# A second iteration written out for each engine, with single context units and the value products ahead of the Toeplitz products

## The reference, cut to what matters

```python
def layernorm(x): return (x - mean(x)) / sqrt(var(x) + 1e-5)
# 1: mixing by Toeplitz matrices, 16 heads of 16 columns
z = softmax(layernorm(x) @ W_A.T / 4, over the rows)         # (512, 16)
v = layernorm(x) @ W_V.T
mix[i, h] = sum over j <= i of z[i - j, h] * v[j, h]         # (512, 256)
x = x + mix @ W_O.T + b_O
# 2: causal attention of the rows on a context given from outside
K, V, Q = ctx @ WK, ctx @ WV, layernorm(x) @ WQ
x = x + softmax(mask(Q @ K.T / 16)) @ V
# 3: a feed-forward part with 2 shared and 16 routed experts, top 2
x = x + shared(layernorm(x)) + routed(layernorm(x))
```

## Time and profile before

| | |
|---|---|
| median of 3 runs | 574.45 us (573.6 to 577.08) |
| the profiled execution | 573.51 us |
| its span, first to last instruction | 571.7 us |
| TensorE busy | 541.9 us, 95% of the span |
| DVE busy | 426.5 us, 75% |
| ScalarE busy | 255.7 us, 45% |
| POOL busy | 191.8 us, 34% |
| TensorE's granted clock | 1.00 throughout |

### The profile page before, as it was taken

How to read it: one execution, slowest core, us unless ns; L and a number is a source line. 1 busy time by engine, 2 the same in 40 slices (tenths; PEclk the granted TensorE clock), 3 DMA queues, 4 the chain that set the end, 5 groups by cost and what they waited for, 6 DMA issues and landing times. The chain is left out here.

```text
span 571.7 us, 12923 instructions
## 1 busy us (share of the span) xinstructions
PE 541.9 (95%) x4716; PEld 368.2 (64%) x4716; DVE 426.5 (75%) x1107; ACT 255.7 (45%) x517; POOL 191.8 (34%) x240
## 2 busy tenths in 40 slices
PE   5787889999999999999999999999999998999997
PEld 4565557566685667766786668666866675666455
DVE  5858687868885787868886888778876776677654
ACT  4565546445354254445344445434543334332332
POOL 4215150223542144223522343234421343133123
PEclk9999999999999999999999999999999999999999
DMA  8995595795439903694449743993189125300351
GB/s 256 308 367 194 182 386 180 155 322 183 112 82 251 335 17 101 148 292 151 111 100 249 242 110 77 204 310 98 51 177 325 57 74 126 64 1 1 86 102 37
DMA packets 90734, 94.70 MB, mean 166 GB/s; under 512 B 28224, under 2 KB 76224, under 8 KB 90432
## 3 DMA queue, kind: packets, MB, share of 16 engines
q1 hardware_dynamic: 90688, 94.09, 58.1%
HBM read 75.66 MB, written 12.12 MB: 154 GB/s over the span
## 5 line engine op out<-in xcount | busy, mean ns | idle before, releaser
L694 POOL TENSOR_TENSOR mid<-gated,mid 128x512 f16<-128x512 f32 x72 | 86.6, 1202 | 214.0 <-ACT mid L880 213.9
L880 ACT ACTIVATE mid<-gated 128x512 f16<-128x512 f32 x72 | 44.9, 624 | 83.3 <-DVEq L1225 80.0
L146 PE MATMUL wide<-w_d,mid 128*128 128x256 f16 x288 | 78.5, 273 | 0.0
L148 PE MATMUL wide<-w_d,mid 128*128 128x256 f16 x288 | 78.5, 273 | 0.0
L147 PE MATMUL wide<-w_d,mid 128*128 128x256 f16 x288 | 78.5, 272 | 0.0
L1203 DVE SCALAR_TENSOR_TENSOR gated<-gated,score 128x512 f32<-128x512 f32 x72 | 49.1, 682 | 37.6 <-ACT gated L875 37.5
L146 PE MATMUL rows<-h3T,w_gu 128*128 128x512 f16 x160 | 60.7, 379 | 0.3 <-DVEq L126 0.3
L146 PE MATMUL score<-h3T,w_gu 128*128 128x512 f16 x160 | 60.7, 379 | 0.2
L147 PE MATMUL rows<-h3T,w_gu 128*128 128x512 f16 x160 | 60.6, 379 | 0.0
L148 PE MATMUL rows<-h3T,w_gu 128*128 128x512 f16 x160 | 60.6, 379 | 0.0
L148 PE MATMUL score<-h3T,w_gu 128*128 128x512 f16 x160 | 60.6, 379 | 0.0
(11 more groups left out here) (249 smaller groups left out, 1402.8 us busy)
## 6 DMA issues: line engine op xcount, KB each, us to landing
toep<-z_scratch SPq DMA_DIRECT2D x14, 2048.0 KB, 18.3
stage<-comb_scratch SPq DMA_DIRECT2D x32, 512.0 KB, 8.5
toep<-z_scratch SPq DMA_DIRECT2D x4, 1024.0 KB, 11.2
x_bo<-in_x SPq DMA_DIRECT2D x8, 512.0 KB, 11.8
x_in<-in_xr SPq DMA_DIRECT2D x7, 512.0 KB, 11.1
qT<-q_scratch SPq DMA_DIRECT2D x7, 512.0 KB, 3.9
vx<-v_scratch SPq DMA_DIRECT2D x7, 512.0 KB, 5.2
out<-x_out SPq DMA_DIRECT2D x7, 512.0 KB, 3.0
```

Source lines behind the costliest of these rows:

```text
L146: pe.matmul(out, stationary[0], moving[0], start=start, stop=False, **kw)
L148: return pe.matmul(out, stationary[1], moving[0], start=False, stop=stop, **kw)
L694: pool.tensor_tensor(mid_slot(j, 1, late), gate_slot(j, late), mid_slot(j, 0, late), ALU.subtract).then_inc(mid_split.sem, 1)
L880: act.activation(mid_slot(j, 0, late), gate_slot(j, late), ACT.Copy).then_inc(mid_hi.sem, 1)
```

## The change

The second iteration leaves the shared `iteration` functions and gets a function of its own, `second_iteration`, on POOL, ScalarE, DVE and TensorE. The tables `CONTEXT_AT` and `CONTEXT_BEFORE` go. The operations are the same, but for these points:

- TensorE makes both value products ahead of the Toeplitz products. Both units (1,2), (1,3) come after the mix turn, units (2,0) to (2,2) ahead of the h2 turn, and the others singly between the steps of the attention; the last two end the iteration, behind the turn of h1.
- The two gate pieces that were last on DVE (numbers `GATES_2` and `GATES_2 + 1`) are made later, and their low half on POOL: a multiplication in place (`w_scaled`) and a subtraction, where DVE used one instruction. ScalarE copies them behind h2T and behind the second exponent, and waits for them one by one.
- The normalisation of x_in for block 2 goes from DVE to ScalarE (`normalise_x`), with its shift made by POOL (`make_shift_x`); the counters' offset is changed to match.
- z's maximum comes earlier on DVE, and x_in's statistics are made in two halves between the attention's steps.
- POOL's list is now: bias, context 2, reciprocal and shift for h2, context 3, the two pieces, context 4, reciprocal and shift for x_in, context 5, the two reciprocals for h3.
- SP loads the residual of block 0 and context 2 ahead of the second gate weights.

In the diff below, the removed branches `if first:` of the shared functions are left out, and `project_mix` loses its second argument.

```diff
--- before.py
+++ after.py
@@ -62,10 +62,6 @@
-CONTEXT_AT = {5: (4, (0, 1)), 6: (4, (2, 3)), 7: (5, (0, 1)), 8: (5, (2,))}
-CONTEXT_BEFORE = {3: (3, (2,)), 4: (3, (3,))}
@@ -280,6 +276,9 @@
...
+        LATE = len(pieces) - LATE_PIECES
+        GATES_2 = LATE - 2
@@ -607,9 +607,10 @@
                 if f and not m:
 
                     sp.wait_ge(first_toep_loaded, 32)
+                    load_residual(it)
+                    load_context(2)
                     load_gates(1)
-                    load_context(2)
-                if f and not d:
+                if f and m and not d:
                     load_residual(it)
                 if f and not m:
                     load_context(3)
@@ -712,8 +713,37 @@
...
+            def part_weights(some):
+                for i in some:
+                    n, k, at = pieces[i]
+                    name, _, dst, _, _ = loads[n]
+                    pool.wait_ge(w_hi, i + 1)
+                    pool.wait_ge(w_lo, i)
+                    src = staged[name][:, k, at]
+                    pool.tensor_scalar(src, src, X_W, None, ALU.mult).then_inc(w_scaled, 1)
+                    pool.wait_ge(w_scaled, i - GATES_2 + 1)
+                    pool.tensor_tensor(dst[:, 1, k, at], src, dst[:, 0, k, at], ALU.subtract).then_inc(w_lo, 1)
+            def second_iteration(it):
+                add_bias(it - 1)
+                part_context_columns(2)
+                reciprocal_deviation(it - 1, 1)
+                make_shift(it - 1)
+                part_context_columns(3)
+                part_weights(range(GATES_2, LATE))
+                part_context_columns(4)
+                reciprocal_deviation(it + 1, 0)
+                make_shift_x(it + 1)
+                part_context_columns(5)
+                reciprocal_deviation(it - 1, 2)
+                reciprocal_deviation(it - 1, 2, 1)
+                if f and m and not d:
+                    second_iteration(it)
+                    return
@@ -925,11 +949,59 @@
...
+            def second_iteration(it):
+                part_context(1, (0, 1))
+                part_weights(range(MIDDLE, GATES_2))
+                for g in range(K2):
+                    take_first_mix(g)
+                part_values(it, it, 0)
+                part_values(it, it, 2)
+                part_turned(it, it - 1, mixT, mixT_hi, "mix")
+                part_context_columns(2)
+                part_context(1, (2, 3))
+                z_powers(it)
+                act.wait_ge(w_lo, GATES_2)
+                part_context(2, (0,))
+                part_context_columns(3)
+                part_context(2, (1,))
+                normalise_last(it - 1, it)
+                part_context(2, (2,))
+                part_turned(it, it - 1, h2T, h2T_hi, "h2")
+                part_weights(range(GATES_2, GATES_2 + 1))
+                part_context(2, (3,))
+                part_z(it)
+                part_context(3, (0,))
+                exp_scores(it, it - 1, 0)
+                exp_scores(it, it - 1, 1)
+                part_weights(range(GATES_2 + 1, LATE))
+                part_context(3, (1,))
+                act.wait_ge(ctx_stored[1], 32)
+                part_prob(it, it - 1, 0)
+                exp_scores(it, it - 1, 2)
+                part_context_columns(4)
+                act.wait_ge(w_lo, GATES_2 + 1)
+                part_context(3, (2,))
+                part_prob(it, it - 1, 1)
+                exp_scores(it, it - 1, 3)
+                part_context(3, (3,))
+                part_prob(it, it - 1, 2)
+                part_context(4, (0,))
+                part_prob(it, it - 1, 3)
+                part_context_columns(5)
+                part_context(4, (1,))
+                act.wait_ge(w_lo, LATE)
+                part_context(4, (2, 3))
+                normalise_x(it + 1)
+                part_turned(it, it - 1, h3T, h3T_hi, "h3")
+                part_context(5, (0, 1))
+                part_turned(it, it + 1, h1T, h1T_hi, "h1")
+                part_context(5, (2, 3))
+                if f and m and not d:
+                    second_iteration(it)
+                    return
@@ -1339,12 +1377,93 @@
...
+            def add_residual(it, k):
+                if not k:
+                    dve.wait_ge(x_biased.sem, x_biased.at(it - 1, 1))
+                    dve.wait_ge(x_kept.sem, x_kept.at(it - 2, 1))
+                rows.take(dve, it, f"o{k}")
+                dve.wait_ge(rows.ready.sem, rows.is_ready(it, f"o{k}"))
+                dve.scalar_tensor_tensor(x_res[:, k:k + 2], rows.bank(f"o{k}")[:].rearrange("p (c e) -> p c e", c=2),
+                                         1 / (X_MIX * X_W), x_bo[:, k:k + 2], ALU.mult,
+                                         ALU.add).then_inc(rows.taken.sem, 1)
+                hold(dve, rows.taken, rows.is_taken(it, f"o{k}"))
+                return statistics(1, x_res, range(k, k + 2))
+            def attended_statistics(it, c):
+                hold(dve, turned.taken, turned.is_taken(it, f"p{c}"))
+                return statistics(2, x_res, [c])
+            def second_iteration(it):
+                b = it - 1
+                rows.take(dve, it, "v0")
+                part_context(1, (0, 1))
+                part_weights(range(MIDDLE, GATES_2))
+                z_max(it)
+                part_values(it, it, 0)
+                part_values(it, it, 2)
+                rows.take(dve, it, "o0")
+                part_turned(it, b, mixT, mixT_hi, "mix")
+                turned.take(dve, it, "h2.0")
+                part_context(1, (2, 3))
+                add_residual(it, 0)
+                aggregate(b, 1, add_residual(it, 2))
+                part_context(2, (0,))
+                normalise(b, it, 1, x_res, h2)
+                z_invert(it)
+                score.take(dve, it, "s0")
+                part_context(2, (1, 2))
+                part_turned(it, b, h2T, h2T_hi, "h2")
+                part_context(2, (3,))
+                part_z(it)
+                part_context(3, (0,))
+                for c in range(2):
+                    score_max(it, b, c)
+                for c in range(2):
+                    score_sum(it, b, c)
+                score.take(dve, it, "s2")
+                part_context(3, (1,))
+                part_prob(it, b, 0)
+                x_statistics(it + 1, range(2))
+                score_max(it, b, 2)
+                score_sum(it, b, 2)
+                score.take(dve, it, "s3")
+                part_context(3, (2,))
+                part_prob(it, b, 1)
+                attended(it, 0)
+                score_max(it, b, 3)
+                score_sum(it, b, 3)
+                attended_statistics(it, 0)
+                part_context(3, (3,))
+                part_prob(it, b, 2)
+                attended(it, 1)
+                x_statistics(it + 1, range(2, C))
+                part_context(4, (0,))
+                part_prob(it, b, 3)
+                aggregate(b, 2, attended_statistics(it, 1))
+                attended(it, 2)
+                part_context(4, (1,))
+                normalise(b, it, 2, x_res, h3)
+                attended(it, 3)
+                attended_statistics(it, 2)
+                aggregate(b, 2, attended_statistics(it, 3), 1)
+                part_context(4, (2,))
+                normalise(b, it, 2, x_res, h3, 1)
+                part_context(4, (3,))
+                for banks in (score, rows):
+                    banks.reach(dve, banks.taken, it)
+                part_turned(it, b, h3T, h3T_hi, "h3")
+                part_context(5, (0, 1))
+                part_turned(it, it + 1, h1T, h1T_hi, "h1")
+                part_context(5, (2, 3))
+                turned.reach(dve, turned.taken, it)
@@ -1745,38 +1827,72 @@
...
+            def second_iteration(it):
+                b = it - 1
+                pe.wait_ge(turned.taken.sem, turned.is_taken(b, "h1.1"))
+                z_product(it)
+                project(it, "v0", h1T, w_v)
+                project(it, "v2", h1T, w_v)
+                pe.wait_ge(ctx_taken.sem, ctx_taken.at(1, 2))
+                for g in range(K2):
+                    toeplitz(it, b, g)
+                pe.wait_ge(mix_taken, K2)
+                turn(it, "mix", h2)
+                context(1, (2, 3))
+                project_mix(it)
+                context(2, (0, 1, 2))
+                turn_halves(it, "h2", h2, h_ready[1], b, h2_normed)
+                context(2, (3,))
+                context(3, (0,))
+                pe.wait_ge(ctx_taken.sem, ctx_taken.at(0, UNITS))
+                pe.wait_ge(turned.taken.sem, turned.is_taken(it, "h2.1"))
+                scores(it, 0)
+                scores(it, 1)
+                context(3, (1,))
+                turn_probs(it, b, 0)
+                scores(it, 2)
+                context(3, (2,))
+                turn_probs(it, b, 1)
+                attend(it, 0)
+                scores(it, 3)
+                context(3, (3,))
+                turn_probs(it, b, 2)
```

(17 more changed lines are left out.)

154 lines of the change are left out of this document (22 added, 132 removed).

## The result

The changed kernel takes **578.86 us** (577.88 to 579.76, 7 runs) against 574.45: ratio 1.0084, 95% interval 1.0066 to 1.0102. It is 0.8% slower where 574.0 was forecast. The two medians alone give 1.0077. The profiled execution has a span of 576.7 us against 571.7.

The account below looks back on a forecast made before the run. TensorE's product queue bounds the kernel; the change reaches only a 61.74 us stretch with 10.8 idle. Gain 1.7 - 0.8 - 0.5 = 0.4 us takes the profiled 573.51 to 573.1; with the median 0.94 above, 574.0 us, range 569.5 to 577.5.

Parts of the forecast that it names:

- the walk: Second iteration followed handover by handover with the old durations: first quarter product at 89.5 instead of 91.19, 1.7 us gained.
- step 6: SBUF port shared by DVE and POOL: z's split waits 0.8 us, POOL's bias delays h3's second normalisation 0.5.
- step 1: Values ahead of Toeplitz: the second load's wait is covered, mix turn starts at 40.3 instead of 41.08, gain 0.8 us.
- step 2: Mix projection: weight pieces gone from DVE there, so it starts at 43.8 without a wait, gain 2.3 us more.
- step 3: Mix projection to the scores: scores start at 55.35, like for like a gain of 4.0 us so far.
- step 4: Scores and attention: TensorE idles 4.5 us where 2.6 before, loss 1.9, gain down to 2.1 us.
- step 5: h3 and the end: POOL's context 5 delays h3's reciprocal, TensorE waits 1.5 and 2.5 us; gain ends at 1.7.
- the 1.0 us break kept: Among the Toeplitz products: the unexplained gap of 1.0 us stays as long as before, Toeplitz ending at 39.4.
- The warning that this break might turn up more: Closing remark on what would be wrong: the unexplained 1.0 us break turning up more often; no chance given.
- 3.1 in all: Running gain in us claimed at the mix projection, from 0.8 for values ahead of Toeplitz and 2.3 more.
- (d): Rival: slow pieces on POOL hold z's split 3.5 us and context 4 by 2: 578.2, over 576, chance 0.12.
- (b): Rival: attention keeps the gain made by the scores, POOL's order costs nothing: 568.7 to 572 us, chance 0.27.

Follow-up runs that it names:

- e5: Changed kernel with the two value products between the two Toeplitz groups instead of ahead of both: 574.57 us, ratio 1.0016 to the kernel before.
- e13: Changed kernel with the edits of e5, e7 and e10, and unit (1,2) between the last Toeplitz product and the mix turn: 569.38 us, ratio 0.9903.
- e12: Kernel before with only the low halves of the two gate pieces moved from DVE to POOL: 575.67 us, ratio 1.0025.
- e4: Kernel before with only the two value products moved ahead of both Toeplitz groups: 576.71 us, ratio 1.0043.
- e11: Changed kernel with the edits of e5, e7 and e10 together: 569.51 us, ratio 0.9900 to the kernel before.
- e10: Changed kernel with context 5's columns made earlier on ScalarE and POOL: 575.33 us, ratio 1.0019 to the kernel before.
- e3: Changed kernel with 20 and 45 idle TensorE products in the two waits of h3: 576.16 us, ratio 1.0038 to the kernel before.
- e8: Changed kernel with the low halves of the two gate pieces given back from POOL to DVE: 580.94 us, ratio 1.0098 to the kernel before.
- e7: Changed kernel with unit (5,0) between the two halves of h3's turn instead of behind it: 575.54 us, ratio 1.0024 to the kernel before.
- e6: Kernel before with the two value products between the two Toeplitz groups: 576.37 us, ratio 1.0054.
- e15: Kernel before with 24 idle products of 256 columns instead of 48 of 128 at TensorE's start: ratio 0.9992.

## Why the prediction was wrong

Measured against the walk (with 0.8 us at the scores and 0.5 at the end for step 6), the first quarter product came at 96.11 instead of 90.8. The 5.3 us are made up of 0.8 at the z product, 1.45 in step 1, 1.7 in step 2, 0.05 in step 3, -1.4 in step 4 and 2.7 in steps 5 and 6. The 0.8 is ahead of every edit: TensorE's 48 idle products at the start took 5.28 us instead of 4.31, and the first z product of block 0 came at 11.20 us instead of 10.39. A z product at 30.11 or later shows in seven of the 17 changed programs' traces, e5 and e13 among them, and e12, made from before, too; so it comes with the execution and not with the change, as far as these traces tell.

- **Step 1, the term "the 1.0 us break kept".** This is the one that failed first. The break was taken as a constant, and the load wait as something to be saved beside it. They were one quantity: 5.3 us from some place ahead, of which the load wait had covered 1.2. Taking that wait away made the break 2.25, and in before, with nothing else changed, 1.90 (e4). The warning that this break might turn up more named the right spot, but it was no rival and had no price.
- **Step 2.** No wait at the projection, as said (0.0 against 1.4 before); what took 5.19 us instead of 3.5 is the half clock, 1.64 us. In e5 and e11 the stage is 3.55, and with e11 the starts are 40.24, 43.79 and 55.39 against the forecast 40.3, 43.8 and 55.35. The walk of this step was right; a term for the clock was missing from it. That the starts agree to 0.1 us is in part luck: in e11 z came 0.2 us late and the break was 0.43 us where the walk had 1.0. The "3.1 in all" of this step counts the 0.8 of step 1 twice (46.16 less 43.8 is 2.4); the later steps go by absolute times, so the sum is free of it.
- **Step 3.** Right to 0.05 us.
- **Step 4.** Waits as named ahead of scores 2 (0.62), scores 3 (1.30) and the last turn (0.77), each 0.2 to 0.4 us less than forecast, and 0.43 instead of 1.0 ahead of the first turn; a loss of 1.3 instead of 1.9.
- **Step 5.** The mechanism is right, shown by e10: POOL's reciprocal starts 0.1 us behind its columns of context 5, and DVE idles 2.65 us. The waits are 1.30 and 3.15 against 1.5 and 2.5. The price was not: at 3.15 us the clock fell, for another 2.3 us. Of the 3.6 us lost in this stage like for like (22.47 against 18.89), 1.3 are left when the clock stays up (20.20 in e3).
- **Step 6.** A piece takes 4.9 us, not 3.3: the subtraction 2.13 as forecast (2.0), but the multiplication 2.79 instead of 1.3, above the upper bound of 2.3. Yet z's split took 0.73 us in its midst, not 0.8 more:

```profile
58.96 2.79 POOL L724 TENSOR_SCALAR stage<-stage 128x1024 f32<-128x1024 f32 x1 [1.50 <-ACT w_gu L796]
...
60.00 0.73 DVE L1335 SCALAR_TENSOR_TENSOR z_parts<-z_exp,z_rsum,z_parts 16x512 f16<-16x512 f32 x1
```

By the rule of the Trainium skill on two SBUF inputs ("SBUF — State Buffer", Who interferes with whom) it should have waited; this row does not show it. The near line rate that the Trainium skill ("GPSIMD Engine Reference", Engine selection) gives for one-input work does not agree either: the one-input instruction took longer than the two-input one. The collision with POOL's bias was there (1.54 us, at 84.09), in step 5's second wait, but no larger than in before (1.64).

**The rivals.** The time of 578.86 is that of (d), 578.2, and a piece was beyond its 4.5 us, but its mechanism did not act: z was not held, and context 4 was ready at 71.34, just ahead of TensorE at 71.40. e8, no faster without the pieces on POOL, excludes it: that the time came out near (d)'s is chance. The time of e11, 569.51, lies in the range of (b) once the break, POOL's order and the clock are out of the way, but not by (b)'s mechanism alone: its attention stage still gives back the 1.3 us of after (14.29).

## What to carry to other kernels

A wait that is taken away can have been the cover of another one that runs from an earlier point: before counting it as saved, ask what else was under way at that time, above all where a gap with no releaser follows close behind it. Waits of TensorE are not worth their length alone: one of 1.9 us and more was in most cases followed by half clock, which cost up to another 2.7 us. Filling it pays beyond its length: a unit of 1.31 us put into its middle gave back 2.6 (e7). Neither is a rule, as the next section shows, so look at the granted clock behind each wait. On a helper that works in order, moving one item ahead of another is only half of the question; the other half is which instruction of its neighbour it will then run beside.

## What was not expected of the hardware

TensorE stopped behind the 342nd product of its program in every run that had a break, for 0.3 to 2.4 us, and went on 2.4 to 2.8 us behind one packet of the queue of instructions. Most waits of 1.9 us and more in this stretch were followed by half clock: 1.90 (e4), 2.25 (after), 2.30 (e12), 2.8 (e10), 3.15 (after), 4.04 (e6). So was that of 1.47 in e15, and 1.30 and 1.07 close together in e7; those of 1.18 and 1.01 in before and of 0.48 and 0.69 in e5 were not. But the length of the wait does not settle it: 2.51 us in e12 left the clock up, and two of about 1.08 and 0.80 close together left it up in before, e4 and e15 and brought it down in e6. A wait of 1.95 us stands ahead of the first z product in all 18 traces, and was followed by half clock in seven of them. What else decides is open. The cost differs between executions of nearly the same program: half clock for 3.5 us in after, for 7 in e10. An in-place multiplication of 128x1024 took POOL 2.79 us, 1.3 times its subtraction of the same size, and DVE has the whole low half in 1.23.
